# A gated cross-attention block whose float32 transpositions read their operands as rounded float32

## The reference

```python
def attention(x, context, Wq, Wk, Wv, Wo, bo):          # 8 heads of 64
    q, k, v = x @ Wq, context @ Wk, context @ Wv         # split into heads
    attn = softmax(q k^T * 64 ** -0.5)                   # 1024 x 77 for each head
    return (attn @ v) @ Wo + bo

def ffn(x, w1, b1, w2, b2):                              # 256 -> 1024 -> 256
    h = quantised(x) @ quantised(w1).T + quantised(b1)
    h = relu(quantised(h))
    return quantised(h) @ quantised(w2).T + quantised(b2)

x = x + tanh(g_xattn[0]) * attention(layernorm(x), ctx, Wq, Wk, Wv, Wo, bo)
x = x + tanh(g_ffn[0]) * ffn(layernorm(x), w1, b1, w2, b2)
```

## Time and profile before

| | us |
|---|---|
| median of 3 runs | 121.85 |
| lowest and highest run | 121.33, 123.11 |
| span of the profiled execution, first to last instruction | 119.5 |
| TensorE busy in the span | 113.6 |
| VectorE busy | 97.7 |
| GpSimd busy | 89.0 |
| ScalarE busy | 76.7 |

### The profile page before, as it was taken

How to read it: one execution, slowest core, us unless ns; L and a number is a source line. 1 busy time by engine, 2 the same in 40 slices (tenths; PEclk the granted TensorE clock), 3 DMA queues, 4 the chain that set the end, 5 groups by cost and what they waited for, 6 DMA issues and landing times.

```text
span 119.5 us, 2896 instructions
## 1 busy us (share of the span) xinstructions
PE 113.6 (95%) x1012; PEld 104.6 (88%) x1012; DVE 97.7 (82%) x223; ACT 76.7 (64%) x169; POOL 89.0 (74%) x160
## 2 busy tenths in 40 slices
PE   7699997999999999999999999999999999999990
PEld 2399975999799999999999999999999999998770
DVE  3039798999999999989999899999797969647981
ACT  4137775968779895995849394848483828448420
POOL 3003678588896988899898959894999998987620
PEclk9999999999999999999999999999999999999999
DMA  3999999100000000000020002000200020020204
GB/s 82 333 251 371 333 388 381 71 0 8 0 3 5 3 0 0 0 5 0 0 88 0 5 0 88 0 8 0 88 0 0 8 88 0 0 87 9 80 14 169
DMA packets 5328, 8.87 MB, mean 74 GB/s; under 512 B 1191, under 2 KB 2242, under 8 KB 5186
## 3 DMA queue, kind: packets, MB, share of 16 engines
q1 hardware_dynamic: 5082, 8.34, 19.8%
q10 hardware_dynamic: 232, 0.34, 0.8%
HBM read 6.59 MB, written 2.10 MB: 73 GB/s over the span
## 4 chain that ended last, share of the span: by engine, by line
PE 90%; DMA 4%; DVE 2%; ACT 1%; issue 1%; SPq 0%; DVEq 0%
PE of_ps L868 24%; PE sc_ps L832 23%; PE h_ps L900 12%; PE of_ps L915 8%; PE tr_ps L844 7%; DMA wk_sb<-in_L_xattn_Wk_dram 4%; PE tr_ps L814 2%; PE h_ps L787 2%; PE tr_ps L915 1%; PE sc_ps L915 1%; PE tr_ps L767 1%; PE of_ps L760 1%; PE tr_ps L760 1%; PE sc_ps L767 1%; DVE x_sb L659 1%; PE of_ps L881 1%
## 5 line engine op out<-in xcount | busy, mean ns | idle before, releaser
L832 PE MATMUL sc_ps<-a_sb,xT 128*128 128x308 f32 x192 | 31.2, 311 | 0.6 <-DVE probs L606 0.6
L868 PE MATMUL of_ps<-u_sb,pT 128*128 128x256 f32 x240 | 30.9, 281 | 0.0
L868 PEld LDWEIGHTS of_ps<-u_sb,pT 128*128 128x128 f32 x240 | 29.5, 188 | 0.1
L832 PEld LDWEIGHTS sc_ps<-a_sb,xT 128*128 128x128 f32 x192 | 27.5, 189 | 1.4 <-issue 1.2
L430 ACT ACTIVATE probs<-probs,rstd 128x616 f32<-128x616 f32 x16 | 13.1, 817 | 23.9 <-DVE probs L606 23.9
L473 ACT ACTIVATE hid_q<-h_ps,b1z 128x256 int8<-128x256 f32 x58 | 24.6, 495 | 3.6 <-PE h_ps L900 3.6
L292 POOL TENSOR_TENSOR probs<-probs,rden 128x616 f32<-128x616 f32 x16 | 19.5, 1221 | 2.0 <-DVE rden L616 2.0
L354 POOL CAST hid<-hid_q 128x512 bf16<-128x512 int8 x27 | 15.8, 611 | 2.0 <-ACT hid_q L473 2.0
L900 PE MATMUL h_ps<-x2T,w1T 128*128 128x256 bf16 x128 | 16.6, 273 | 0.1
L601 DVE TENSOR_REDUCE mx<-sc_ps 128x8 f32<-128x616 f32 x16 | 12.6, 787 | 4.1 <-PE sc_ps L832 4.1
L900 PEld LDWEIGHTS h_ps<-x2T,w1T 128*128 128x128 bf16 x128 | 12.4, 98 | 1.7 <-ACT x2T L479 0.3
(11 more groups left out here) (123 smaller groups left out, 177.4 us busy)
## 6 DMA issues: line engine op xcount, KB each, us to landing
w_sb<-in_L_ffn_w_dram SPq DMA_DIRECT2D x2, 1024.0 KB, 10.9
out_dram<-x_sb SPq DMA_DIRECT2D x7, 256.0 KB, 2.5
x_sb<-in_x_dram SPq DMA_DIRECT2D x4, 256.0 KB, 7.7
x_sb<-in_x_dram SPq DMA_DIRECT2D x1, 1024.0 KB, 9.7
wq_sb<-in_L_xattn_Wq_dram SPq DMA_DIRECT2D x1, 512.0 KB, 5.2
wv_sb<-in_L_xattn_Wv_dram SPq DMA_DIRECT2D x1, 512.0 KB, 7.4
wo_sb<-in_L_xattn_Wo_dram SPq DMA_DIRECT2D x1, 512.0 KB, 8.4
wk_sb<-in_L_xattn_Wk_dram SPq DMA_DIRECT2D x1, 256.0 KB, 4.2
```

What stands on the lines that cost most here:

```text
L832: ins = nc.tensor.matmul(sc_ps[:, a, 0:HALF], xT[:, T % 2, p, c, :], a_sb[:, q, T // TB, c, HALF * a:HALF * a + HALF], start=first, stop=last)
L868: ins = nc.tensor.matmul(attn_ps, pT[:, T % 2, p, P * c:P * c + P], u_sb[:, q, MC * (T // TB) + c, :], start=first, stop=last)
```

## The change

A second name is given to the storage of the query weights, of the centred rows and of the probabilities. It has the type float32r, so TensorE reads the same words as rounded float32. A helper allocates the tensor under the second name, releases it and allocates the first name in its place. The identity is cast to that type by one more GpSimd instruction, ahead of the bf16 cast. The transpositions take the second names, the new identity and an output seen as float32r. `consts` is raised once more, so two waits on it count one higher, and TensorE waits on it once more before the query weights. The instructions that write the tensors under the first name, and those that read the PSUM results, are unchanged.

```diff
+        def words_of(name, shape):
+            with nc.sbuf_tensor(name + "_words", shape, F32R) as words:
+                pass
+            return words, sb(name, shape)
...
-        wq_sb = sb("wq_sb", [P, DK, INNER])
+        wq_words, wq_sb = words_of("wq_sb", [P, DK, INNER])
...
+        ident_r = sb("ident_r", [P, P], F32R)
...
-        xn = sb("xn", [P, 2, D])
+        xn_words, xn = words_of("xn", [P, 2, D])
...
-        probs = sb("probs", [P, 2, HMP])
+        probs_words, probs = words_of("probs", [P, 2, HMP])
...
             pool.wait_ge(ident_set, 1)
+            nc.gpsimd.tensor_copy(ident_r[:, :], ident[:, :]).then_inc(consts, 1)
             nc.gpsimd.tensor_copy(ident_b[:, :], ident[:, :]).then_inc(consts, 1)
...
-                    pool.wait_ge(consts, 2)
+                    pool.wait_ge(consts, 3)
...
-                    ins = nc.tensor.transpose(xT_ps[:, P * c:P * c + P], xn[:, T % 2, P * c:P * c + P], ident[:, :])
+                    ins = nc.tensor.transpose(xT_ps[:, P * c:P * c + P].bitcast(F32R), xn_words[:, T % 2, P * c:P * c + P],
+                                              ident_r[:, :])
...
-                    ins = nc.tensor.transpose(pT_ps[:, P * c:P * c + P], probs[:, T % 2, P * c:P * c + P], ident[:, :])
+                    ins = nc.tensor.transpose(pT_ps[:, P * c:P * c + P].bitcast(F32R), probs_words[:, T % 2, P * c:P * c + P],
+                                              ident_r[:, :])
...
-                pe.wait_ge(consts, 1)
+                pe.wait_ge(consts, 2)
...
             pe.wait_ge(wq_in, 16)
+            pe.wait_ge(consts, 1)
             for j in range(PAIRS):
                 for c in range(DK):
-                    ins = nc.tensor.transpose(q_banks[j][:, P * c:P * c + P], wq_sb[:, c, P * j:P * j + P], ident[:, :])
+                    ins = nc.tensor.transpose(q_banks[j][:, P * c:P * c + P].bitcast(F32R), wq_words[:, c, P * j:P * j + P],
+                                              ident_r[:, :])
...
-                    ins = nc.tensor.transpose(of_ps[:, 0, D * T + P * c:D * T + P * c + P], xn[:, T, P * c:P * c + P], ident[:, :])
+                    ins = nc.tensor.transpose(of_ps[:, 0, D * T + P * c:D * T + P * c + P].bitcast(F32R),
+                                              xn_words[:, T, P * c:P * c + P], ident_r[:, :])
```

## The result

The changed kernel took 119.87 us as the median of four runs (119.53 to 120.06), the kernel before 121.59 us beside it (121.02 to 123.11): a ratio of 0.9879 with a 95% interval of 0.9843 to 0.9915. Repeated later with more runs (experiment 2) it was 119.98 against 121.86 us, ratio 0.9838 (0.9785 to 0.9890). So the change brings 1.2 to 1.6%, 1.7 to 1.9 us by the medians. The forecast was 118.6 us, 2.6%. The direction and the range held, the size was about twice too large. The forecast had set about 2% as what can be told from no change, with 0.56 on faster: the first measurement lies under that line, and the interval of the second reaches across it. (Runs more than 1.5% above the fastest of their kernel are in the medians and ranges here, not in the ratios.)

A forecast was written before the change was run, and what follows sets the result against it. TensorE was taken to lead until 19 us, level with VectorE (GpSimd close) until 61 us, then alone setting the pace. Savings of 0.43 + 0.28 + 2.51 = 3.22 us, say 3.2, from 121.85 gave 118.6 us, range 117.5 to 122.0.

The forecast's parts named there:

- The price of a transposition: All 120 transpositions of 128 columns: 66 ns each under the rounded name instead of 110, saving 44 ns.
- rival B: Each transposition gains only half, settling at 83 ns, a saving of 27 ns: 119.7 us; chance 0.25.
- steps 5 and 6: Twelve faster transpositions give 0.53 us, but GpSimd's widened hidden values let only 0.28 us through.
- Up to 19 us: Query weights and first rows, where TensorE leads the chain: 0.43 us saved.
- From 19 to 45 us: VectorE full, GpSimd's scaling the gate: 37 faster transpositions only make TensorE wait longer; 0.04 us credited.
- Step 7 to the end: TensorE stays the bound, by little, so 57 transpositions at 44 ns bring 2.51 us.
- C: The rounded name gains nothing per transposition, records stay at 274 ns: 121.85 us, at worst 122.6; chance 0.15.
- D: Slower, since no rounded product in the trace is narrow; records near 380 ns would prove it; chance 0.12.

The follow-up runs named there:

- experiment 2: The changed kernel again, unaltered, with more runs against the kernel before: 119.98 us, ratio 0.9838.
- experiment 9: Kernel without the block, copying x; series of 32 equal TensorE operations with wide bf16 products between: rounded transposition 90 ns, rounded product of 128 columns 116 ns.
- experiment 1: Kernel without the block, copying x; series of 48 equal TensorE operations: transpositions 109 ns plain, 87 rounded, 56 bf16.
- experiment 6: Kernel before, with eight widenings of hidden values moved from GpSimd to ScalarE: 121.28 against 121.19 us, ratio 1.0017.
- experiment 5: Changed kernel, with eight widenings of hidden values (tiles 4 to 11) moved from GpSimd to ScalarE: 119.55 us, ratio 0.9861.
- Experiment 7: Changed kernel, with ScalarE's copy of the transposed second rows in step 6 put ahead of its rounding of the hidden layer: 119.28 us, ratio 0.9848.
- experiment 8: Changed kernel, with eight widenings moved from GpSimd to ScalarE and ScalarE's step 6 copy of transposed second rows put first: 119.42 us, ratio 0.9854.
- experiment 3: Rounded names only for the transpositions up to step 6, plain ones after, against the kernel before: 121.56 against 121.86 us, ratio 0.9960.
- late kernel: Rounded names only for the transpositions from step 7 on, plain ones earlier, against the kernel before: 121.07 us, ratio 0.9895.

## Why the forecast went wrong in size

**The price of a transposition (the step that failed).** The forecast took 66 ns, from the surcharge of wide rounded products over their stream. It had no term for the load. The 117 ns of 256 columns, read as 107 ns of stream and 10 of surcharge, are just as near to the 115 and 116 ns of 64 and 128 columns (experiment 9), where the load sets the distance, so this row could not tell the two apart. At 128 columns the identity's one pass takes 62 ns at most (experiment 1, 64 columns loaded), and the load comes forward: 85 ns in the kernel, 87 and 90 in the series. The saving is 25 ns by the chain's pieces, not 44. The rows even held the warning that rival B quoted, 188 ns of load record against 140; yet the load record of the rounded transposition is 141 ns like the plain one's, so that was not the right sign for it either. From `attend(6)` to `attend(14)` the kernel before takes 100.99 - 54.93 = 46.06 us, the kernel after 99.59 - 55.02 = 44.57: 1.49 us for 52 transpositions, 29 ns each. With that the 57 late ones are worth 1.65 us, not 2.51. Rival B's 83 ns was close to the right price, at its chance of 0.25, and its ground, a load that does not get faster, is the right kind. But it took the number as halfway between 56 and 110 ns, which nothing measured supports; that it came out near is luck. So in part is its 119.7 us against 119.87, since it counts the 0.28 us of steps 5 and 6, which did not come.

**Up to 19 us.** The forecast had 0.43 us. From the start of the query transpositions to the mark the kernel before takes 19.16 - 7.17 = 11.99 us, and 12.05 in experiment 6. The changed kernel takes 11.77, 11.83, 12.00, 11.81 and 11.82 (after, experiments 2, 5, 7, 8). The mean gain is 0.17 us. The steps of the forecast with 25 ns in the place of 44 give 0.28, and this is too small a difference to follow in traces whose starts differ. In the first trace of the changed kernel the query transpositions also started 0.33 us later than in that of before, for a transfer (timelines of TensorE, before and after), so that it shows no gain at the mark at all:

```profile
7.17 0.60 PE L966 MATMUL of_ps<-ident,wq_sb 128*128 128x128 f32 x4
```

```profile
7.50 0.54 PE L977 MATMUL of_ps<-ident_r,wq_sb_words 128*128 128x128 f32 x4 [0.85 <-DMA wq_sb<-in_L_xattn_Wq_dram]
```

**From 19 to 45 us.** The forecast's text credits 0.04 us, which its sum leaves out, and nothing came (experiment 3). The idle time rose from 0.83 to 1.48 us and is released by the two engines named; at 44 ns each it was to reach about 1.6.

**Steps 5 and 6.** The forecast let 0.28 us through GpSimd's widened values, and that much did pass: counted from the mark, the scores in this step start at 53.15 - 19.16 = 33.99 us before and at 52.97 - 19.27 = 33.70 after. It missed the next gate, ScalarE's copy. The kernel before (timelines of ScalarE and TensorE):

```profile
54.32 0.46 ACT L479 CAST x2T<-of_ps 128x256 bf16<-128x256 int8 x1
```

```profile
53.15 1.95 PE L832 MATMUL sc_ps<-a_sb,xT 128*128 128x308 f32 x12
54.93 1.99 PE L868 MATMUL of_ps<-u_sb,pT 128*128 128x256 f32 x15
```

The copy ends at 54.78 us, and the product follows 0.15 us later, as it follows 0.14 later in the kernel after. There was no slack, so the product of tile 6 gained 35.77 - 35.75 = 0.02 us. Experiment 7 opened the gate: 0.24 us at the product, 0.33 at the end. In the kernel before the product came 1.78 us behind the start of the scores, and 1.81 in kernel 7, where nothing holds it: the gate did not yet cost anything there, by the trace alone.

**Step 7 to the end.** That TensorE stays the bound held for steps 7 to 14. The last transpositions did not: GpSimd, with no wait from 81.6 to 107.5 us, holds `probsT(15)`, and of a due gain of 0.14 us the step makes a loss of 0.12. Experiment 5 gave that back. The forecast had asked whether GpSimd's work fits in one step, and took it that only the variance step makes some steps longer. But in steps 11 to 13 GpSimd also adds the output bias of two tiles instead of one, and step 11 has both (timeline of GpSimd, kernel after):

```profile
83.34 1.22 POOL L300 TENSOR_TENSOR probs<-probs,rden 128x616 f32<-128x616 f32 x1
...
86.76 1.41 POOL L383 TENSOR_TENSOR x_sb<-x_sb,b_gated 128x256 f32<-128x256 f32 x2
...
89.98 1.22 POOL L300 TENSOR_TENSOR probs<-probs,rden 128x616 f32<-128x616 f32 x1
```

From one scaling to the next it takes 6.64 us there, where TensorE's step takes 5.83. Up to 81.62 us GpSimd still waits for VectorE now and then, so it does not fall behind all along. What it has in hand is the time from the end of a scaling to TensorE's transposition of it. In the kernel after this is 1.56, 0.63, 0.76 and 0.05 us for tiles 12 to 15, in the kernel before 1.87, 1.04, 1.33 and 0.38. Two steps use it up: step 11, and TensorE's step 14, which has no scores and lasts 3.87 us (99.59 - 95.72), where GpSimd needs 4.85 from the scaling of tile 14 to that of 15 (100.34 - 95.49). The change took the rest.

**The sum.** 0.17 + 0 + 0 + 1.41 = 1.58 us, against 1.7 and 1.9 by the medians. Of the 3.22 us of the forecast 0.86 were the price in the late part, 0.26 the start, 0.28 the missed gate, and 0.24 GpSimd at the end (1.65 - 1.41, where experiment 5 measured 0.28): 1.64 us in all.

**Rivals C and D.** C would have kept the records at 274 ns; they fell to 251. D's ground, that a narrow rounded product falls to four passes, is refuted by experiment 9: 116 ns at the full clock, where it had 219. The rounded product of 128 columns costs half of the plain one.

The Trainium skill (TensorE: Matmul & The Clock Gate, LDWEIGHTS (loading the stationary operand)) gives a weight load as its columns over 1.2 GHz, whatever the rows: 107 ns for 128 columns, 53 for 64. For rounded products the distances of the series come near, with 116 and 66 ns, 9 and 13 above. They do not for other forms, where 128 loaded columns went at 56 ns (bf16), 64 ns (plain float32 transposition) and 84 to 90 ns (rounded transposition). Its 81 ns for pairs (Back-to-back issue gap) names no type; it is near the 85 found here, but bf16 pairs were at 56.

## What to carry to other kernels

A price for a narrow operation cannot be taken from a wide one by subtracting the stream: ask which of load and stream the row was bound by, and measure the pair at the size in question. Before crediting a lead at a stage's end, list every wait of the next long operation with its slack; the tightest decides, and here it was not the first one found. When the bound engine gets 4% quicker and two others have work for 91 and 94% of its step, compare their steps with its new ones one by one, not a mean or a typical one: here two uneven steps near the end used up what GpSimd had in hand. The cure was to move work off it, and that was worth nothing before the change (experiments 5 and 6).

## What the runs showed of the hardware

**The granted clock in a long series of transpositions.** In experiment 1 TensorE ran only transpositions from 17.11 us on, busy all the time. Stretches of that kernel (window, length, PE, PEld and POOL busy, granted clock):

```profile
40.00:41.00 1.00, 1.00 (x18) 1.00 (x16) 0.00 (x0) 1.00 0.00 0
...
43.00:46.00 3.00, 3.00 (x25) 2.99 (x24) 0.00 (x0) 0.50 0.00 0
...
69.00:73.00 4.00, 4.00 (x35) 4.00 (x34) 0.00 (x0) 1.00 0.00 0
```

The clock was at 2.4 GHz to 41 us, after series of transpositions only, and at 1.2 GHz from 42 to 67, through rounded products of 64 and 128 columns at 219 ns each. It rose again between 68 and 69 us, in the series of rounded products of 256 columns. With wide products between the series (experiment 9) it stayed at 1.00 from 10 to 70 us. The Trainium skill (TensorE: Matmul & The Clock Gate, Part 4: PE-mode transpose) says that the full clock does not engage for transpositions, which do not count as busy in the same way. The fall agrees; that the clock stayed at 1.00 through the first 24 us of transpositions does not quite. In the kernel, where 8 of the 51 operations of a step are transpositions, it stays at 1.00.

**Two starts.** From one group of four records of the keys' products to the next it is 0.52 us in some executions and 1.03 in others. One stretch, 6 to 7 us, of the kernel before and of the late kernel (PE, PEld, DVE, ACT, POOL busy, granted clock):

```profile
6.00:7.00 1.00, 1.00 (x10) 1.00 (x9) 0.00 (x0) 0.00 (x0) 0.00 (x0) 1.00 0.86 164
```

```profile
6.00:7.00 1.00, 1.00 (x6) 1.00 (x6) 0.00 (x0) 0.00 (x0) 0.00 (x0) 1.00 0.84 164
```

Ten records against six in the same microsecond, the transfers alike, and a granted clock of 1.00 in both. It puts the mark at 20.8 instead of 18.4 to 19.3 us, more than the whole change brings. The pace is that of half the clock, but the row does not say so; the cause stays open. It is why the rests were compared and not the spans.
